# Cross-attention and expert FFN on one core: casts moved to GpSimd, attention's steps reordered, stack copies in 2 KB runs

## The chip, the core and the metric

The kernel runs on one core of a Trainium2 chip. Its engines are TensorE (PE, matrix multiply into PSUM), VectorE (DVE), ScalarE (ACT), GpSimd (POOL) and SyncE (SP, which here issues nearly all plain transfers). Each engine runs its own list of instructions in order and waits on semaphores. The metric is device time in microseconds for one launch, as the median of several runs.

## The reference

`x` and the context are (8, 512, 256), 16 heads of 16, hidden size 682, 8 experts of which each token takes 2.

```python
def xattn(x, k, v, w, b):            # k = v = context
    q = split(x) / 16 ** 0.25; k = split(k) / 16 ** 0.25
    p = softmax(einsum('bthd,bshd->bhts', q, k))
    return merge(einsum('bhts,bshd->bthd', p, v)) @ w.T + b
def ffn(x, Wg, W1, W2, W3):
    logits = x @ Wg.T
    gate = softmax(where(in_top_2(logits), logits, -inf))
    h = silu(einsum('bsd,ehd->bseh', x, W1)) * einsum('bsd,ehd->bseh', x, W2)
    return einsum('bsed,bse->bsd', einsum('bseh,edh->bsed', h, W3), gate)
x = x + xattn(layernorm(x), ctx, ctx, w_proj, b_proj)
x = x + ffn(layernorm(x), Wg, W1, W2, W3)
```

## The kernel before

**Numbers.** Many operands stand as two f16 parts: a high part (the value rounded to f16) and a low part (value minus high part, again f16). The normalised queries, the keys, the normalised rows `z` for the FFN and the expert weights are all split so. For each the high part is a copy with a cast, and the low part a subtraction behind it.

**Attention.** The eight batches go through a software pipeline of *slots*, 16 (`PER`) for a batch, each in two halves. Batch b's slot s stands at slot 16b + s; what is due for it at a constant `AT_...` (counted from its first slot, negative for what is prepared ahead) is issued when every engine's loop comes to that slot. So steps of three or four batches stand side by side in one stretch of 16 slots, which I call a frame. In a half slot PE makes the transposed scores of the batch eight slots behind (line 1284, for the exponential), the scores of the current batch (line 1271, for the row maximum), and, in the first half, four products of probabilities and values (line 1299); then at most one *misc* step: a transpose or small product whose half slot stands in `HALF_MISC`. ACT takes the exponential of 128x1024 (line 842); DVE takes the maximum of 128x1024 (line 973). Both read from three pairs of PSUM banks that the score products take in turn: a product waits for the reader of the product three before it. `max` is the misc step that transposes the maxima of a quarter of a batch (line 1313); ACT then copies them to `max_row` (line 859) and SP moves them into row 48 of each stack.

**Stacks.** The score products contract over `q_stack` and `k_stack`: three blocks of 16 rows (high, high and low part against high, low and high) in partitions 0 to 47 for the even heads and 64 to 111 for the odd ones, each row 8 pairs of heads x 512. Twelve transfers a batch (`k_part`, line 492, and `q_part`, line 497) copy them there from `k16` and `qt16` on SP's queue. Batch b's first score product waits for all twelve (line 1271's block).

**POOL's list.** In a frame POOL does, in this order of slots (mod 16): `pick_slots` (1), `inverse_root` for x (2), `scatter` with its 8 indirect transfers (2, line 474), `split_weights` 0 (3), `inverse_root` for z (4), low part of q (5), `split_weights` 1 (7), low part of z and its copy (8, lines 805 and 809), low part of the keys (12, line 694), `choose` (12, lines 700 to 718), `split_weights` 2 (14, lines 749 to 759). ACT makes the high part of the keys (line 914, slot 14), of q (line 927) and of z (line 931, slot 8). `choose` gives `sel16`, for which PE's misc step `prefix` waits (line 1352, slot 15).

**SP's list.** In the frame: weights out and the next weights in (slots 1, 9, 13), `x_in` and `v_ext` (5), `kt_in` and the keys' six stack transfers (10, both behind POOL's low keys), q's six (12), the maxima (2, 6, 10, 14), `x_res` and `x2` (0).

**FFN.** 36 tiles of 256 slots: gathered rows, three products for each pair of parts. The first six tiles (`EARLY`) are cut in 12 pieces each and stand in the half slots from 272 on, beside the last batch's attention; the others follow in plain loops. POOL adds each tile's two halves to the output with an indirect transfer (`add_rows`, line 769); for the early tiles those stand in its list at fixed half slots: tile 0's at 288 and 292 (slots 144 and 146).

Of the kernel before, what the change touches and what calls it, by code (L numbers as in the profile page):

```python
# [9 lines left out]
F16 = mybir.dt.float16  # L10
# [88 lines left out]
AT_CHOOSE = 44  # L99
# [4 lines left out]
AT_K_LO = -4  # L104
AT_K_PARTS = -6
AT_MAX_ROW = 2
AT_PICK = 49
AT_Q_HI = -13
AT_Q_LO = -11
AT_Q_PARTS = -4  # L110
AT_SCATTER = 50
AT_V_IN = 5
AT_WEIGH = 12
AT_W_LO = (3, 7, 14)
# [4 lines left out]
AT_X_RES = 16  # L119
AT_X_ROOT = -14  # L120
AT_Z_HI = 40
AT_Z_LO = 40
# [3 lines left out]
STEP_PREP = (-98, -96, -94, -92, -79)  # L126
# [3 lines left out]
HALF_MISC = sorted([(-23, 'turn_q', 0), (-20, 'turn_q', 1), (10, 'max', 0), (16, 'max', 1), (24, 'max', 2), (33, 'max', 3), (39, 'heads', 0), (43, 'heads', 1), (49, 'heads', 2), (55, 'turn', 0), (57, 'heads', 3), (59, 'turn', 1), (61, 'project', 0), (63, 'project', 1), (66, 'project', 2), (69, 'project', 3), (77, 'turn_z', 1), (79, 'turn_z', 0), (83, 'logits', 0), (85, 'turn_l', 0), (94, 'prefix', 0)])  # L130
# [140 lines left out]
def build(nc, xq_l, x_l, v_l, kT_l, wp_l, bias, wg_l, w12_l, w3_l, const, out):  # L271
    ctx = ExitStack()
    with ctx:
# [25 lines left out]
        run = sb("run", [P, E])  # L299

# [105 lines left out]
        s_small = sem("s_small")  # L406
        s_cst = sem("s_cst")
# [73 lines left out]
        def _(sp):  # L481
# [7 lines left out]
            def k_part(b, j, part):  # L489
                for par in range(2):  # L490
                    row = 64 * par + j * D
                    sp.dma_start(k_stack[b % 2][row:row + D, :, :], k16[part][:, par, :]).then_inc(s_kd, 16)

            def q_part(b, j, part):
                for par in range(2):
                    row = 64 * par + j * D
                    sp.dma_start(q_stack[b % 2][row:row + D, :, :], qt16[part][:, par, :]).then_inc(s_qd, 16)
# [174 lines left out]
        def _(pool):  # L672
# [112 lines left out]
            for slot in range(FIRST, LAST):  # L785
                for b in due(slot, AT_K_LO):
                    if b >= 1:
                        low_keys(b)
# [14 lines left out]
                for b in due(slot, AT_Z_LO):  # L803
                    pool.wait_ge(s_zh, b + 1)
# [26 lines left out]
        def _(act):  # L831
            act.wait_ge(s_con, 16)
# [64 lines left out]
            for slot in range(FIRST, LAST):  # L897
# [13 lines left out]
                for b in due(slot, AT_K_HI):  # L911
                    act.wait_ge(s_kin, (b + 1) * 16)
                    ge(act, s_kd, b * 96)
                    nc.scalar.copy(k16[0][:, :, :], kt_in[:, :, :]).then_inc(s_kh, 1)
# [13 lines left out]
                for b in due(slot, AT_Z_HI):  # L928
                    act.wait_ge(s_zn, (b + 1) * NT)
                    ge(act, s_sc, b * 128)  # L930
                    nc.scalar.copy(z_row[:, 0, :, 0:W // 2].bitcast(F16), z_n[:, :, :]).then_inc(s_zh, 1)
# [546 lines left out]
```

## Time and profile before

| | |
|---|---|
| median of 3 runs | 873.97 us (872.97 to 878.98) |
| the profiled execution | 874.99 us, span 873.1 us |
| PE busy | 784.8 us (90%) |
| DVE busy | 602.1 us (69%) |
| ACT busy | 557.6 us (64%) |
| POOL busy | 439.6 us (50%) |
| DMA queue of SP | 92448 packets, 148.76 MB, 60.0% of 16 engines |
| mean granted clock of PE | 0.992 |

Busy time is the time in which an engine ran an instruction; PE's matmuls overlap each other, and their ends are modelled. In the rows below, a time behind a group is the engine's idle time just before the instruction, with what ended it; "issue" is a wait that the profile puts down to nothing.

### The profile page before, as it was taken

What the parts mean: (1) busy time and instruction counts of PE and PEld (TensorE: products, weight loads), DVE (VectorE), ACT (ScalarE), POOL (GpSimd) and SP (SyncE); (2) the same over time, 40 slices, a digit from 0 to 9 for tenths busy, and PEclk for the clock granted to TensorE, in tenths of its full rate; (3) what the DMA queues carried; (4) which work ended last, traced back from release to release, by engine and by line L of the source; (5) the groups of instructions that cost most, each with busy time, mean ns of one, the idle gap of its engine ahead of it and who ended that gap; (6) DMA issues with size and microseconds to landing.
All of it is one profiled execution on the core that took longest, in us unless ns stands there. A gap on an engine that the chain in (4) does not pass through costs nothing.

```text
span 873.1 us, 20010 instructions
## 1 busy us (share of the span) xinstructions
PE 784.8 (90%) x6472; PEld 481.2 (55%) x6472; DVE 602.1 (69%) x1224; ACT 557.6 (64%) x970; POOL 439.6 (50%) x431
## 2 busy tenths in 40 slices
PE   0578898989989899897989899999999999999995
PEld 0112233333333333332326788888888888888884
DVE  4888888979888898899924557555555555555553
ACT  3369789888897988966884454444444444444442
POOL 4555435786777868675643665222224222222222
PEclk9999999999999999999999999999999999999998
DMA  8575756866659685674266699999997699383832
GB/s 184 179 191 167 202 124 225 188 217 157 189 209 188 215 170 190 182 161 169 106 195 225 190 252 299 293 308 271 267 261 160 161 250 255 57 251 49 250 41 25
DMA packets 105959, 167.57 MB, mean 192 GB/s; under 512 B 54688, under 2 KB 83232, under 8 KB 101280
## 3 DMA queue, kind: packets, MB, share of 16 engines
q1 hardware_dynamic: 92448, 148.76, 60.0%
q0 software_dynamic: 13440, 17.90, 10.6%
q8 instruction: 39, 0.64, 0.3%
q14 instruction: 32, 0.26, 0.1%
HBM read 119.75 MB, written 42.55 MB: 186 GB/s over the span
## 4 chain that ended last, share of the span: by engine, by line
PE 48%; ACT 2%; issue 1%; POOL 1%; DMA 0%; DVE 0%; POOLq 0%; ACTq 0%; DVEq 0%
PE ps L1376 10%; PE ps L1378 10%; PE ps L1380 10%; PE ps L1394 4%; PE ps L1396 4%; PE ps L1398 4%; PE ps L1299 2%; ACT probs L842 1%; PE ps L1403 1%; PE ps L1284 1%; POOL slots L474 1%; ACT z_n L847 1%; PE ps L1327 0%; PE ps L1338 0%; PE ps L1271 0%
## 5 line engine op out<-in xcount | busy, mean ns | idle before, releaser
L973 DVE TENSOR_REDUCE neg_max<-ps 128x2 f16<-128x1024 f32 x256 | 309.1, 1221 | 37.6 <-PE ps L1271 32.9
L842 ACT ACTIVATE probs<-ps 128x1024 f32<-128x1024 f32 x256 | 259.0, 1024 | 61.7 <-PE ps L1284 61.2
L769 POOL DMA_INDIRECT out<-y,aim x72 | 113.4, 1574 | 237.6 <-DVE y L1202 160.0
L1376 PE MATMUL ps<-zt,w 128*128 128x256 f16 x792 | 216.0, 273 | 1.4 <-issue 1.3
L1378 PE MATMUL ps<-zt,w 128*128 128x256 f16 x792 | 215.9, 273 | 0.0
L1380 PE MATMUL ps<-zt,w 128*128 128x256 f16 x792 | 215.9, 273 | 0.0
L876 ACT ACTIVATE silu<-ps 128x256 f32<-128x256 f32 x216 | 82.7, 383 | 183.4 <-PE ps L1380 173.8
L1183 DVE SCALAR_TENSOR_TENSOR hid<-ps,silu 128x256 f32<-128x256 f32 x216 | 91.7, 425 | 136.0 <-ACT silu L876 128.3
L1299 PE MATMUL ps<-probs,v_ext 128*32 128x512 f32 x1024 | 138.7, 613 | 5.3 <-ACT heads L910 4.4
L1271 PE MATMUL ps<-k_stack,q_stack 48*128 48x512 f16 x512 | 104.3, 406 | 35.4 <-ACT probs L842 17.8
L1284 PE MATMUL ps<-q_stack,k_stack 49*128 49x512 f16 x512 | 101.9, 396 | 7.3 <-DVE neg_max L973 7.1
L1394 PE MATMUL ps<-w,hid 128*128 128x256 f16 x360 | 98.1, 273 | 0.0
L1396 PE MATMUL ps<-w,hid 128*128 128x256 f16 x360 | 98.1, 273 | 0.0
L1398 PE MATMUL ps<-w,hid 128*128 128x256 f16 x360 | 98.1, 273 | 0.0
L1284 PEld LDWEIGHTS ps<-q_stack,k_stack 49*128 49x128 f16 x512 | 24.7, 93 | 113.0 <-issue 79.9
L1376 PEld LDWEIGHTS ps<-zt,w 128*128 128x128 f16 x792 | 77.5, 98 | 15.0 <-issue 5.3
L1378 PEld LDWEIGHTS ps<-zt,w 128*128 128x128 f16 x792 | 77.5, 98 | 9.0
L1380 PEld LDWEIGHTS ps<-zt,w 128*128 128x128 f16 x792 | 77.5, 98 | 9.0
L1190 DVE TENSOR_TENSOR hid<-hid 128x256 f16<-128x256 f32 x180 | 76.3, 424 | 1.3
L884 ACT CAST hid<-hid 128x256 f16<-128x256 f32 x180 | 72.0, 400 | 6.0 <-DVE hid L1183 2.4
L474 POOL DMA_INDIRECT slots<-z_row,slot_u x64 | 63.2, 987 | 24.4 <-issue 20.2
L759 POOL TENSOR_TENSOR w_lo<-w_in,w_hi 128x1408 f16<-128x1408 f32 (+1 forms) x24 | 70.7, 2946 | 2.0
(126 smaller groups left out, 908.0 us busy)
## 6 DMA issues: line engine op xcount, KB each, us to landing
w<-w_parts SPq DMA_DIRECT2D x36, 1408.0 KB
w<-w_parts SPq DMA_DIRECT2D x36, 768.0 KB
w_in<-in_w SPq DMA_DIRECT2D x16, 704.0 KB, 6.0
v_ext<-in_v SPq DMA_DIRECT2D x8, 1024.0 KB, 5.6
k_stack<-k SPq DMA_DIRECT2D x48, 128.0 KB, 5.3
q_stack<-qt SPq DMA_DIRECT2D x48, 128.0 KB, 5.0
w_in<-in_w SPq DMA_DIRECT2D x8, 768.0 KB, 5.0
w_parts<-w_hi SPq DMA_DIRECT2D x16, 352.0 KB, 2.3
```

The costliest lines, as they stand in the source:

```text
L769: nc.gpsimd.indirect_dma_start(out=out, out_offset=bass.IndirectOffsetOnAxis(ap=aim[frm][:, t, 0:1].bitcast(U32), axis=0), in_=y[frm][:, t ...
L842: nc.scalar.activation(probs[g % 2][:, j:j + 2, k, :], pair_banks[PLACE["exp", u] % 3], ACT.Exp, scale=0.25).then_inc(s_exp, 1)
L973: nc.vector.tensor_reduce(neg_max[b % 2][:, i, c:c + 3:2], pair_banks[PLACE["max", u] % 3], AX.X, ALU.max, negate=True).then_inc(s_red, 1)
L1271: mm = nc.tensor.matmul(to[:, par, :], q_stack[r][rows, a, i * P:(i + 1) * P], k_stack[r][rows, a, :], start=True, stop=True)
L1284: mm = nc.tensor.matmul(to[:, par, :], k_stack[r][rows, a, k * P:(k + 1) * P], q_stack[r][rows, a, :], start=True, stop=True)
L1299: mm = nc.tensor.matmul(pv_bank[32 * n:32 * n + 32, :], v_ext[b % 2][:, j, 4 * g + n, :], probs[g % 2][:, n, j, :], start=(j == 0), stop=( ...
L1376: nc.tensor.matmul(dst, w[:, kk, 1, cols], z16[:, kk, :], start=(kk == 0), stop=False)
L1378: nc.tensor.matmul(dst, w[:, kk, 0, cols], z16[:, 2 + kk, :], start=False, stop=False)
L1380: mm = nc.tensor.matmul(dst, w[:, kk, 0, cols], z16[:, kk, :], start=False, stop=(kk == 1))
L1394: nc.tensor.matmul(y_bank[t], h[1], w3[par][:, 0, m, :], start=first, stop=False, skip_group_check=True)
L1396: nc.tensor.matmul(y_bank[t], h[0], w3[par][:, 1, m, :], start=False, stop=False, skip_group_check=True)
L1398: nc.tensor.matmul(y_bank[t], h[0], w3[par][:, 0, m, :], start=False, stop=False, skip_group_check=True)
```

## The change

- The high part of the keys (batches 1 to 7) and of z (all batches) is made by POOL, just ahead of the low part, and no longer by ACT.
- POOL's order in a frame: `inverse_root` for x at slot 13 (was 2, in the frame after), low q 6 (was 5), high and low keys 9 (was 12, low alone), high and low z 10 (was 8, low alone), `split_weights` 2 at 12 (was 14), `choose` and `pick_slots` 15 (were 12 and 1 of the next frame).
- The misc step `max` 3 stands at half slot 32 (was 33).
- Two statistics of x on DVE move by one or more quarter slots, and the aggregate by one.
- `v_ext` and `x_res` are due a slot later and a slot earlier on SP; no other transfer of SP stands between the old place and the new.
- The host lays the keys and queries out so that two pairs of heads lie side by side in a partition: each stack transfer reads 64 partitions in runs of 2 KB (was 128 in runs of 1 KB).
- ACT runs one exponential of 128x1 before anything else.

```diff
-AT_CHOOSE = 44
+AT_CHOOSE = 47
-AT_K_LO = -4
+AT_K_LO = -7
-AT_PICK = 49
+AT_PICK = 47
-AT_Q_LO = -11
+AT_Q_LO = -10
-AT_V_IN = 5
+AT_V_IN = 6
-AT_W_LO = (3, 7, 14)
+AT_W_LO = (3, 7, 12)
-AT_X_RES = 16
-AT_X_ROOT = -14
-AT_Z_HI = 40
-AT_Z_LO = 40
+AT_X_RES = 15
+AT_X_ROOT = -19
+AT_Z_LO = 42
-STEP_PREP = (-98, -96, -94, -92, -79)
+STEP_PREP = (-98, -97, -93, -91, -78)
-HALF_MISC = sorted([... (33, 'max', 3), ...])
+HALF_MISC = sorted([... (32, 'max', 3), ...])
...
-                    sp.dma_start(k_stack[b % 2][row:row + D, :, :], k16[part][:, par, :]).then_inc(s_kd, 16)
+                    sp.dma_start(k_stack[b % 2][row:row + D, :, :], k16[part][64 * par:64 * par + 64, :, :]).then_inc(s_kd, 16)
...
                 for b in due(slot, AT_K_LO):
                     if b >= 1:
+                        pool.wait_ge(s_kin, (b + 1) * 16)
+                        ge(pool, s_kd, b * 96)
+                        nc.gpsimd.tensor_copy(k16[0][:, :, :], kt_in[:, :, :]).then_inc(s_kh, 1)
                         low_keys(b)
...
                 for b in due(slot, AT_Z_LO):
+                    pool.wait_ge(s_zn, (b + 1) * NT)
+                    ge(pool, s_sc, b * 128)
+                    nc.gpsimd.tensor_copy(z_row[:, 0, :, 0:W // 2].bitcast(F16), z_n[:, :, :]).then_inc(s_zh, 1)
                     pool.wait_ge(s_zh, b + 1)
...
         def _(act):
+            act.wait_ge(s_zero, 1)
+            nc.scalar.activation(warm_up[:, :], ones16[:, 0:1], ACT.Exp).then_inc(s_warm, 1)
+            act.wait_ge(s_warm, 1)
...
-                for b in due(slot, AT_Z_HI):
-                    act.wait_ge(s_zn, (b + 1) * NT)
-                    ge(act, s_sc, b * 128)
-                    nc.scalar.copy(z_row[:, 0, :, 0:W // 2].bitcast(F16), z_n[:, :, :]).then_inc(s_zh, 1)
...
-    x_q = np.asarray(x).reshape(B, T, PAIRS, 2, D).transpose(0, 1, 3, 4, 2)
+    x_q = np.asarray(x).reshape(B, T, PAIRS // 2, 2, 2, D).transpose(0, 1, 3, 4, 5, 2)
```

## Rows read from the trace of the kernel before

**Rows 1.** Busy time by stretch; columns: stretch, length, PE, PEld, DVE, ACT, POOL, PEclk, DMA.

```profile
257.50:310.57 53.07, 48.28 (x370) 16.98 (x370) 46.80 (x80) 45.70 (x59) 40.19 (x45) 1.00 0.71 195
...
528.00:858.00 330.00, 328.61 (x3002) 292.80 (x3001) 178.93 (x472) 158.41 (x427) 103.39 (x67) 1.00 0.81 207
```

**Rows 2.** What PE waited for, 26.7 to 460 us: total, times, longest.

```profile
PE ps L1271 <- ACT probs L842: 17.8, 38, 1.5
...
PE ps L1271 <- DMA q_stack<-qt: 1.0, 1, 1.0
PE ps L1271 <- issue: 0.9, 2, 0.7
```

**Rows 3.** Timeline of PE over a frame's end and the next one's start: start, length.

```profile
273.89 0.19 PE L1352 MATMUL ps<-sel,upper 128*128 128x32 f16 x1
...
277.04 0.39 PE L1271 MATMUL ps<-k_stack,q_stack 48*128 48x512 f16 x2 [0.66 <-issue]
...
278.90 0.39 PE L1313 MATMUL ps<-ident,neg_max 128*4 128x128 f16 x4
...
279.87 0.39 PE L1271 MATMUL ps<-k_stack,q_stack 48*128 48x512 f16 x2 [0.27 <-ACT probs L842]
...
283.78 0.39 PE L1271 MATMUL ps<-k_stack,q_stack 48*128 48x512 f16 x2 [0.69 <-ACT probs L842]
```

**Rows 4.** Timeline of ACT in the same frame.

```profile
254.47 1.03 ACT L931 CAST z_row<-z_n 128x1024 f16<-128x1024 f32 x1
...
280.20 0.56 ACT L859 COPY max_row<-ps 4x512 f16<-4x512 f16 x1
```

**Rows 5.** Timeline of POOL in the same frame.

```profile
250.12 2.87 POOL L759 TENSOR_TENSOR w_lo<-w_in,w_hi 128x1408 f16<-128x1408 f32 x1
255.58 2.14 POOL L805 TENSOR_TENSOR z_row<-z_n,z_row 128x1024 f16<-128x1024 f32 x1 [2.59 <-ACT z_row L931]
...
258.90 2.12 POOL L694 TENSOR_TENSOR k<-kt_in,k 128x1024 f16<-128x1024 f32 x1
263.10 0.19 POOL L700 CAST top_f<-top_e 128x8 f32<-128x8 uint32 x1 [2.08 <-DVE top_e L1018]
...
265.44 1.48 POOL L749 TENSOR_SCALAR w_in<-w_in 128x1536 f32<-128x1536 f32 x1
...
272.30 1.04 POOL L723 TENSOR_TENSOR ediff<-con,diff 128x4 f32<-128x4 f32 x1
...
275.16 0.20 POOL L681 TENSOR_TENSOR rstd<-mv,con 128x4 f32<-128x4 f32 x1
...
276.95 0.20 POOL L736 CAST z_row<-con 128x8 uint32<-128x8 f32 x1
```

**Rows 6.** Groups by line and shape: a cast on POOL; busy, mean ns, idle before.

```profile
L752 POOL CAST w_hi<-w_in 128x1408 f16<-128x1408 f32 x16 | 21.7, 1357 | 1.1
```

**Rows 7.** Timeline of SP and of POOL: loads of the third weights, and one's arrival.

```profile
97.85 0.47 SPq L502 DMA_DIRECT2D w_in<-in_w  x1
...
103.36 1.47 POOL L749 TENSOR_SCALAR w_in<-w_in 128x1536 f32<-128x1536 f32 x1 [12.21 <-DMA w_in<-in_w]
...
255.81 0.46 SPq L502 DMA_DIRECT2D w_in<-in_w  x1
```

**Rows 8.** Start of the program: timelines of ACT and DVE.

```profile
6.92 1.28 ACT L914 ACT_TABLE_LOAD   x1 [6.92 <-DMA kt_in<-in_k_t]
...
24.82 1.41 DVE L980 BATCH_NORM_STATS2 stats<-x_in 128x6 f32<-128x256 f32 x4 [9.06 <-DMA x_in<-in_x_q]
```

**Rows 9.** DMA view of 8 to 27 us: GB/s in 40 slices of 0.475 us.

```profile
GB/s 398 393 323 261 59 57 224 203 168 155 147 110 145 127 136 123 125 136 127 144 106 149 114 151 106 160 112 140 136 188 103 164 371 414 423 440 347 382 380 128
```

**Rows 10.** Last batch beside the early FFN tiles: timelines of POOL and of PE.

```profile
494.91 1.63 POOL L769 DMA_INDIRECT out<-y,aim  x1 [0.30 <-issue]
495.94 0.85 POOL L681 TENSOR_TENSOR rstd<-mv,con 128x4 f32<-128x4 f32 x1
...
500.72 0.52 PE L1338 MATMUL ps<-con,z_n 128*128 128x128 f32 x3 [1.86 <-ACT z_n L847]
```

More of the change, by code:

```diff
@@ L129 @@
 STEP_TOP_INDEX = 173
-HALF_MISC = sorted([(-23, 'turn_q', 0), (-20, 'turn_q', 1), (10, 'max', 0), (16, 'max', 1), (24, 'max', 2), (33, 'max', 3), (39, 'heads', 0), (43, 'heads', 1), (49, 'heads', 2), (55, 'turn', 0), (57, 'heads', 3), (59, 'turn', 1), (61, 'project', 0), (63, 'project', 1), (66, 'project', 2), (69, 'project', 3), (77, 'turn_z', 1), (79, 'turn_z', 0), (83, 'logits', 0), (85, 'turn_l', 0), (94, 'prefix', 0)])
+HALF_MISC = sorted([(-23, 'turn_q', 0), (-20, 'turn_q', 1), (10, 'max', 0), (16, 'max', 1), (24, 'max', 2), (32, 'max', 3), (39, 'heads', 0), (43, 'heads', 1), (49, 'heads', 2), (55, 'turn', 0), (57, 'heads', 3), (59, 'turn', 1), (61, 'project', 0), (63, 'project', 1), (66, 'project', 2), (69, 'project', 3), (77, 'turn_z', 1), (79, 'turn_z', 0), (83, 'logits', 0), (85, 'turn_l', 0), (94, 'prefix', 0)])
 FIRST, LAST = -27, PER * (B - 1) + 51
@@ L299, in build @@
         run = sb("run", [P, E])
+        warm_up = sb("warm_up", [P, 1])
         att = ctx
@@ L406, in build @@
         s_small = sem("s_small")
+        s_warm = sem("s_warm")
         s_cst = sem("s_cst")
@@ L496, in q_part @@
                     row = 64 * par + j * D
-                    sp.dma_start(q_stack[b % 2][row:row + D, :, :], qt16[part][:, par, :]).then_inc(s_qd, 16)
+                    sp.dma_start(q_stack[b % 2][row:row + D, :, :], qt16[part][64 * par:64 * par + 64, :, :]).then_inc(s_qd, 16)
             def load_weights(e, c):
@@ L911, in _ @@
                 for b in due(slot, AT_K_HI):
-                    act.wait_ge(s_kin, (b + 1) * 16)
-                    ge(act, s_kd, b * 96)
-                    nc.scalar.copy(k16[0][:, :, :], kt_in[:, :, :]).then_inc(s_kh, 1)
+                    if b == 0:
+                        act.wait_ge(s_kin, 16)
+                        nc.scalar.copy(k16[0][:, :, :], kt_in[:, :, :]).then_inc(s_kh, 1)
                 for i in range(NT):
@@ L1437 @@
     c = np.asarray(ctx_1024)
-    x_q = np.asarray(x).reshape(B, T, PAIRS, 2, D).transpose(0, 1, 3, 4, 2)
-    k_t = c.reshape(B, T, PAIRS, 2, D).transpose(0, 4, 2, 3, 1).reshape(B, P, 2, T)
+    x_q = np.asarray(x).reshape(B, T, PAIRS // 2, 2, 2, D).transpose(0, 1, 3, 4, 5, 2)
+    k_t = c.reshape(B, T, PAIRS // 2, 2, 2, D).transpose(0, 4, 5, 2, 3, 1).reshape(B, P, 2, T)
     v = np.zeros((B, P, NT, H, 32), np.float32)
```

## The prediction

> **What bounds the kernel now.** I read the stretches first. From 528 us to the end PE is busy 328.61 of 330 us: the FFN tiles run at PE's pace, and nothing in this change touches them [rows 1]. All that can move lies before. A steady attention frame, 257.5 to 310.57 us, has PE busy 48.28 of 53.07 us, DVE 46.80, ACT 45.70 and POOL 40.19 [rows 1]. So PE is the bound there as well, with 4.8 us of idle time in a frame; a faster ACT or a busier POOL matters only where PE waits for it. Then I read what PE waited for: 17.8 us for exponentials in 38 waits, 1.0 us for `q_stack`, 0.9 us in two waits that the profile calls issue [rows 2]. Last I read the frame's timelines, for the place of each wait and the slack of each engine's list [rows 3 to 5].
>
> **The change, part by part.** The sum is made against the profiled execution (874.99 us), which lies 1.0 us above the median of the three runs (873.97 us); the forecast is given against the median.
>
> *Casts off ACT.* ACT loses two casts of about 1.03 us in a frame [rows 4]. They pay only where an exponential is late for PE. The cast of z stands at 254.47 us and the keys' one 17 us behind it; PE's waits for exponentials in this frame stand at 279.87 us (0.27 us) and 283.78 us (0.69 us), in half slots where no misc step separates two score products, and there ACT itself had been waiting for PE [rows 3, 4]. What hides the casts is ACT's own slack, 7.4 us of 53.07 [rows 1]. I take 0. Other frames could hold some of it: the far end is all of the 17.8 us [rows 2], the near end is 0.
>
> *Casts onto POOL.* Two casts of 1024 at 1357 ns for 1408 [rows 6] are 0.99 us each, 2 us in a frame of which POOL idles 12.9 [rows 1]. The question is what is queued behind. PE's `prefix` at 273.89 us [rows 3] waits for `choose`, which now stands behind `split_weights` 2 and `inverse_root`. Worked from POOL's times [rows 5]: `split_weights` 1 ends at 250.12 + 2.87 = 252.99. High and low keys, 0.99 + 2.12, end at 256.1; high z, 0.99, and low z with its copy, 258.90 - 255.58 = 3.32, end at 260.4. The third weights are asked for at 255.81; the same load asked for at 97.85 had POOL working at 103.36, 5.5 us later [rows 7], so they are here at 261.3. The split takes 272.30 - 265.44 = 6.9, to 268.2; `inverse_root` 276.95 - 275.16 = 1.8, to 270.0; `choose` 265.44 - 263.10 = 2.3, to 272.3. That is 1.6 us ahead of `prefix`: cost 0. If the cover is gone, each us of lateness is one us of PE in each of six frames. `pick_slots` waits for DVE behind `prefix` in both orders, so `scatter` gains at most `inverse_root`'s 1.8 us, and the z root behind it waits for DVE's statistics: worth 0.
>
> *`max` 3 from half slot 33 to 32.* The second half slot of slot 0 is now empty. A score product of the following half must wait for the exponential begun in this one. With the transposes between (278.90 us) the wait at 279.87 was 0.27 us; with nothing between, as in the next slot, it is 0.69 us at 283.78 [rows 3]. PE's work is the same, so the step costs 0.42 us. The copy of the maxima (0.56 us, at 280.20 [rows 4]) also moves from behind that exponential to ahead of it; the transposes end shortly before the product, so I add 0.1 of it. That is 0.5 us in a frame. It happens for batches 0 to 6; batch 7's has no score product beside it, and batch 6's falls where DVE builds the tile table and is late anyway, so I count six: +3.0 us. Ends: 0, if later waits absorb it, and 7 x (0.42 + 0.56) = 6.9.
>
> *Statistics of x, `v_ext`, `x_res`.* DVE's pieces move by a quarter slot or two past one maximum, whose result PE needs two half slots later; the transfers pass no other. 0.
>
> *Keys' transfers earlier.* POOL finishes the low keys at 256.1 instead of 258.90 + 2.12 = 261.0 [rows 5]; SP has just asked for the third weights (255.81 [rows 7]), so the keys' six leave some 4.7 us earlier and are through before q's six, which stay where they are behind the second maxima. The wait at 277.04 (0.66 us, called issue [rows 3]) is that of a batch's first score product, like the 1.0 us for `q_stack` [rows 2]. Both issue waits go: -0.9 us. The 1.0 us is batch 1's, whose keys were not late: it stays. Ends: 0 and -1.9.
>
> *2 KB runs.* At the start the queue carries stack packets alone from its seventh to its thirty-second slice. The first two slices reach 224 and 203 GB/s, then the rate falls to between 103 and 188, about 130, though the packets are the same size; `x_in` behind them runs at 371 to 440 [rows 9]. A cost for each packet would hold from the first slice on, so I read a limit on bytes at the rows that are written, and take 0. The other end is a doubled rate: q's six transfers (786 KB at 130 GB/s, 6.0 us) in 3.0 us, with batch 1's `x_in`, for which DVE waits until 24.82 us [rows 8], 2.6 us earlier beyond the next term, and the 1.0 us of batch 1 gone: -3.6 us together.
> By the Trainium skill, page "SBUF — State Buffer", section "Door 1: The DMA port swizzle", sixteen neighbouring partitions reach only 4 of the 16 ports of 27.2 GB/s, 109 GB/s for one transfer whatever its runs; that page speaks against this edit, its sum is +3.2 us where a price for each packet would give -0.4, and the slices near 130 GB/s, with two transfers overlapping, agree with it.
>
> *Early exponential.* The table load (1.28 us at 6.92 us [rows 8]) moves ahead of the keys' arrival, so the high keys are ready 1.28 us earlier. The normalised q is not, as it waits for POOL. The queue is at 59 and 57 GB/s in slices five and six [rows 9], nearly 1 us that the keys can fill; q's transfers then meet less backlog. -0.3 us, ends 0 and -0.8.
>
> *The adds of the first FFN tile.* `pick_slots` of batch 6 moves from slot 145 to 143, past the add at slot 144, and holds it until PE's `prefix` is done. The add then stands between the pick and `scatter`. One add takes 495.94 - 494.91 = 1.03 us up to the next operation, which takes 0.85 instead of 0.20 us [rows 5, 10]: 1.0 to 2.0 us, and I take 1.4. Behind `scatter` come tile 0's second add and batch 7's root, for which ACT's z and PE wait, at 500.72 already for 1.86 us [rows 10]: +1.4 us.
>
> Sum: 0 + 0 + 3.0 + 0 - 0.9 + 0 - 0.3 + 1.4 = +3.2 us: 878.2 us against the profiled execution, 877.2 us as a median.
>
> **The rivals.**
> *ACT was the hidden bound.* Then the waits for exponentials (17.8 us [rows 2]) shrink with its load. For it: 38 waits are on ACT. Against: those shown stand where ACT had idled. If 8 to 18 us go and the rest of the sum holds, 869 to 859 us. Chance 0.12, of which 0.08 below 865.2.
> *The stack copies double their rate.* -3.6 on the sum: 873.6 us. For it: packets were at the highest rate when few were in flight. Against: the fall within a microsecond [rows 9]. Chance 0.18.
> *The moved `max` 3 is absorbed* by the frame's other waits: +0.2, 874.2 us. Chance 0.10.
> *`choose` comes too late (slower).* Its place is `prefix`. It decides once `split_weights` 2 starts later than 261.3 + 1.6 = 262.9 us: a load of 7.1 us instead of 5.5, now that the keys' transfers leave right behind it. A cast at the subtraction's price (2.1 us) would bring POOL itself only to 262.7. Two us over are 6 x 2 = 12 us: 889 us; one is 883. Chance 0.10.
> *Main case*, 873 to 881 us. Chance 0.50.
>
> **How the numbers follow.** The likeliest case gives 877.2 us. About 1% (8.7 us) is what a measurement of this kernel can tell from no change. Faster than 865.2 takes the larger part of the first rival and a little for what I don't see: 0.10. Slower than 882.7 takes nearly all of the late `choose` and a little of the main case's upper bounds (6.9 + 2.0): 0.11. Within 1%: 0.79. The range 868 to 883 us holds the main case, the doubled copies, the absorbed step and the edge of the other two.
>
> **What would show it.** In the changed kernel: the score product of half slot 2 waits about 0.7 to 0.8 us for an exponential in every frame; no issue wait at a batch's first score product from batch 2 on; stack packets of 2 KB take about twice as long and the DMA rate in 12 to 20 us stays near 130 GB/s; DVE starts on batch 1's statistics at about 24.5 us; `prefix` never waits for POOL; PE's wait for batch 7's z is near 3.3 us. I am wrong if PE's waits for exponentials fall by several us, if the early stack copies end 2 us sooner, or if `prefix` waits.

## The result, and the profile after

| | before | after |
|---|---|---|
| median (4 runs each, same chip) | 874.42 us (872.97 to 878.98) | 885.65 us (883.39 to 887.93) |
| ratio, 95% interval | | 1.0105 [1.0081, 1.0130] |
| the profiled execution, its span | 874.99 us, 873.1 us | 886.15 us, 884.3 us |
| PE busy | 784.8 us | 787.2 us |
| ACT / POOL busy | 557.6 / 439.6 us | 543.9 / 453.5 us |

The change costs 11.2 us, where 3.2 were forecast. The span (first to last instruction of the profiled execution) grew by 11.2 us too, so the two traces hold the whole loss.

**Where it is.** I looked first for the place. The last group of products of probabilities and values stands at the same point of the work in both kernels, at the end of the steady attention. Timelines of PE, of the kernel before and then of the changed one (start, length):

```profile
470.72 1.06 PE L1299 MATMUL ps<-probs,v_ext 128*32 128x512 f32 x8
```

```profile
471.27 1.07 PE L1305 MATMUL ps<-probs,v_ext 128*32 128x512 f32 x8
```

So at the start of that group the changed kernel is 0.55 us behind, and 10.7 us are lost after it. I call what follows this group the *tail*: 402.4 us of the span before, 413.0 after. Busy time by stretch there (columns as in [rows 1]), before and after:

```profile
500.00:520.00 20.00, 19.28 (x195) 17.11 (x196) 10.68 (x38) 11.57 (x30) 13.35 (x18) 1.00 0.99 247
520.00:540.00 20.00, 20.00 (x185) 17.93 (x184) 16.77 (x56) 10.01 (x27) 11.88 (x13) 1.00 1.04 308
```

```profile
499.00:502.50 3.50, 0.41 (x4) 0.12 (x2) 0.00 (x0) 2.04 (x5) 1.27 (x3) 1.00 0.96 287
502.50:505.90 3.40, 3.22 (x15) 2.52 (x16) 1.92 (x5) 2.57 (x8) 0.00 (x0) 0.50 0.87 297
505.90:523.00 17.10, 14.19 (x140) 12.20 (x137) 8.46 (x31) 7.24 (x19) 10.06 (x8) 1.00 0.77 185
523.00:529.80 6.80, 3.96 (x29) 2.93 (x30) 1.85 (x9) 0.00 (x0) 5.12 (x16) 0.50 0.78 253
540.00:858.00 318.00, 316.51 (x2892) 282.13 (x2891) 172.29 (x453) 152.45 (x412) 96.03 (x62) 1.00 0.83 211
```

PE idles in two places and then runs at a granted clock of 0.50 (1.2 GHz instead of 2.4) for 3.4 and 6.8 us. From 540 us on the tiles run as before. What PE waited for from 460 us on (total, times, longest), the two longest of after; the longest of before was the 1.86 us for `z_n` of [rows 10]:

```profile
PE ps L1358 <- POOL sel L717: 5.7, 1, 5.7
PE ps L1344 <- ACT z_n L857: 3.3, 1, 3.3
```

**The bill.** `prefix` of batch 7 waits 5.75 us for the `sel16` of `choose`. The wait for `z_n` is 3.27 us instead of 1.86 [rows 10]: +1.4. In a half-clock stretch the work takes twice its time, so half the busy time is lost: 3.22 / 2 = 1.6 and 3.96 / 2 = 2.0, an estimate. Together 10.8 us, of 10.7.

**How it comes about.** Timeline of POOL in the changed kernel; the adds are those of tile 0 (483.61 and 496.89), tile 1 (507.29 and 509.22) and tile 2 (520.03 and 521.92). In [rows 10] tile 0's second add starts at 494.91 us.

```profile
482.83 0.46 POOL L732 TENSOR_TENSOR pick<-hot,pos 128x32 f32<-128x32 f32 x2 [5.15 <-DVE pos L1048]
483.61 1.81 POOL L770 DMA_INDIRECT out<-y,aim  x1 [0.32 <-issue]
...
496.89 1.61 POOL L770 DMA_INDIRECT out<-y,aim  x1 [0.30 <-issue]
...
507.29 1.63 POOL L770 DMA_INDIRECT out<-y,aim  x1 [6.86 <-issue]
509.22 1.56 POOL L770 DMA_INDIRECT out<-y,aim  x1 [0.30 <-issue]
...
520.03 1.58 POOL L770 DMA_INDIRECT out<-y,aim  x1 [4.79 <-DMA out<-y,aim]
521.92 1.53 POOL L770 DMA_INDIRECT out<-y,aim  x1 [0.30 <-issue]
522.89 0.76 POOL L701 CAST top_f<-top_e 128x8 f32<-128x8 uint32 x1
...
525.45 0.25 POOL L717 TENSOR_TENSOR sel<-hot 128x32 f16<-128x32 f32 x1
```

The first lines are the foreseen step: the pick waits 5.15 us with tile 0's first add behind it, and the scatter and the second add follow 2.0 us later than before (1.4 us, if the 0.55 us by which all of it is behind is taken off). The rest was not foreseen. Timeline of SP, before and then after: the loads of w1 and w2 (1.4 MB each) and, at 498.71 us, one of w3 (768 KB):

```profile
496.46 0.36 SPq L546 DMA_DIRECT2D w<-w_parts  x1
```

```profile
496.64 0.36 SPq L547 DMA_DIRECT2D w<-w_parts  x1
498.71 0.34 SPq L557 DMA_DIRECT2D w<-w_parts  x1
...
509.62 0.34 SPq L547 DMA_DIRECT2D w<-w_parts  x1
```

The second add starts at 496.89 us, 0.25 us *behind* the load; in the kernel before it started 1.55 us ahead of it (494.91 against 496.46). I call this distance the add's *lead*. The DMA view of the changed kernel, of 498 to 502 us and then of 502 to 506 us, splits the packets by queue (hardware_dynamic is SP's, software_dynamic is GpSimd's). The last two fences give the add's time from issue to landing, after and then before:

```profile
q1 hardware_dynamic: 92, 1.04, 93.8%
```

```profile
q1 hardware_dynamic: 182, 1.08, 66.5%
q0 software_dynamic: 143, 0.13, 20.6%
```

```profile
out<-y,aim POOLq DMA_INDIRECT x1, 9.6
```

```profile
out<-y,aim POOLq DMA_INDIRECT x1, 4.2
```

From 498 to 502 us not one packet of the add moves. From 502 to 506 us its packets (143 of 1 KB or less) share the time with the last 27 of the 1.4 MB load, of 11 KB each, and with 126 of the w3 load, of 6 KB. It lands 9.6 us after its start, against 4.2 us in the kernel before. Tile 1's adds wait for it (`add_rows` waits for all adds of the tile before) and start at 507.29 us. The second of them, at 509.22 us, is 0.4 us *ahead* of the next load, and that is not enough: the view of 511 to 514 us has no packet of GpSimd's queue, and 520.03 us is when POOL goes on, with the add landed. `choose` of batch 7 stands behind tile 2's adds, because the change moved it from slot 156 to 159. Its input, the indices that DVE finds, was complete at 515.3 us, 4.8 us before PE went idle for it:

```profile
515.12 0.16 DVE L1024 FIND_INDEX8 top_e<-top,logit 128x8 uint32<-128x8 f32 x1
```

In the kernel before, `choose` stood ahead of tile 2's adds; its `sel16` was ready at 514.1 us, 2.3 us before `prefix`.

**The other steps.** PE's waits over the attention, 26 to 460 us, after (compare [rows 2]): exponentials take 2.9 us more, and no issue wait at a batch's first score product is left.

```profile
PE ps L1277 <- ACT probs L852: 20.7, 35, 1.5
```

PE in the half slots of `max` 3 and of the next slot (compare 279.87 and 283.78 in [rows 3]), and the start of the program on ACT and DVE (compare [rows 8]):

```profile
277.37 0.39 PE L1277 MATMUL ps<-k_stack,q_stack 48*128 48x512 f16 x2 [0.81 <-ACT probs L852]
...
281.28 0.39 PE L1277 MATMUL ps<-k_stack,q_stack 48*128 48x512 f16 x2 [0.69 <-ACT probs L852]
```

```profile
0.71 1.28 ACT L840 ACT_TABLE_LOAD   x1 [0.71 <-PEq L1476]
...
6.97 1.04 ACT L924 CAST k<-kt_in 128x1024 f16<-128x1024 f32 x1 [4.77 <-DMA kt_in<-in_k_t]
```

```profile
24.11 1.41 DVE L986 BATCH_NORM_STATS2 stats<-x_in 128x6 f32<-128x256 f32 x4 [8.12 <-DMA x_in<-in_x_q]
```

### The profile page after: what moved, and what is told of

The parts are those of the page before. It is cut to its first block and busy times, and to the rows that moved or that the text cites. A ratio compares the mean times of both kernels' runs of the same rounds, so it can differ in the third digit from the quotient of the medians.

```text
span 884.3 us, 20011 instructions
## 1 busy us (share of the span) xinstructions
PE 787.2 (89%) x6472; PEld 483.5 (55%) x6472; DVE 602.1 (68%) x1224; ACT 543.9 (62%) x956; POOL 453.5 (51%) x446
## 5 line engine op out<-in xcount | busy, mean ns | idle before, releaser
L1277 PE MATMUL ps<-k_stack,q_stack 48*128 48x512 f16 x512 | 104.2, 406 | 35.4 <-ACT probs L852 20.7
L1290 PEld LDWEIGHTS ps<-q_stack,k_stack 49*128 49x128 f16 x512 | 24.7, 93 | 109.0 <-issue 69.1
```

The costliest lines, as they stand in the source:

```text
L1277: mm = nc.tensor.matmul(to[:, par, :], q_stack[r][rows, a, i * P:(i + 1) * P], k_stack[r][rows, a, :], start=True, stop=True)
L1290: mm = nc.tensor.matmul(to[:, par, :], k_stack[r][rows, a, k * P:(k + 1) * P], q_stack[r][rows, a, :], start=True, stop=True)
```

## The experiments

The theory: the two moved steps `pick_slots` (batch 6) and `choose` (batch 7), among the adds of the first tiles, are the loss; casts, stack runs and `max` 3 play no part in it. Ratios are to the kernel before on the same chip, with 95% intervals. The kernel before itself ran between 872.5 and 882.3 us in these comparisons, so differences of 2 us between versions are at the edge of what they can tell. In the diffs `B - 1` is batch 7 and `B - 2` batch 6; the other batches stay where the changed kernel has them.

**1. `choose` of batch 7 alone at its old slot**

```diff
                 for b in due(slot, AT_CHOOSE):
-                    choose(b)
+                    if b < B - 1:
+                        choose(b)
+                for b in due(slot, 44):
+                    if b == B - 1:
+                        choose(b)
```

> The changed kernel with one thing put back: batch 7's choose stands at its old slot (156), ahead of the two adds of FFN tile 2, which wait for earlier adds to land. Theory (choose of batch 7 is caught behind adds whose landing is 8 to 10 us late): PE's wait of 5.75 us at prefix goes, and with it the 6.8 us at half clock right behind it, worth 3.4 us; PE's wait for batch 7's z (3.3 us) stays. Time 875 to 879 us against 885.7 for the changed kernel. Rival 1 (POOL is overloaded by the casts, so it would be late with choose wherever it stands): prefix still waits 2 to 5 us, 881 to 885 us. Rival 2 (the loss is spread over attention's frames): no change, 885 us.

Measured 879.91 us, ratio 1.0041 [1.0014, 1.0069]. Batch 7's `prefix` no longer waits for POOL, and the wait for `z_n` stays at 3.3 us. PE waits 1.8 us for heads behind it, and 6.8 us at half clock follow with PE busy for 6.1 of them, where 3.4 us had followed in the changed kernel; the forecast had no such stretch left, and its 879 us were just missed. With `pick_slots` late, `choose`'s place is worth some 0.6% of the 1.05. Neither of the expected rivals' times came (881 to 885, 885 us).

**2. `pick_slots` of batch 6 alone at its old slot**

```diff
                 for b in due(slot, AT_PICK):
-                    pick_slots(b)
+                    if b != B - 2:
+                        pick_slots(b)
+                for b in due(slot, 49):
+                    if b == B - 2:
+                        pick_slots(b)
```

> The changed kernel with another thing put back: batch 6's pick_slots stands at slot 145 again, behind tile 0's first add. Theory: the scatter and tile 0's second add start about 2 us earlier, the add gets ahead of the 1.4 MB weight load of an FFN tile instead of behind it and lands in about 5 us instead of 10; PE's wait for z falls from 3.3 to about 1.9 us; tile 1's and 2's adds are earlier, so batch 7's choose, though still behind tile 2's adds, is late by 1 to 4 us instead of 5.75. Time 876 to 882 us. Rival 1 (POOL's casts): the wait for z stays near 3.3 us and the time near 885. Rival 2 (spread over the frames): 885 us.

Measured 876.95 us, ratio 1.0009 [0.9983, 1.0034]: the loss is gone with this step alone, though `choose` still stands late. So the two steps don't add up: `choose` is late only when the adds are. Timeline of POOL and SP: the second add starts 1.5 us ahead of the load and lands after 4.5 us, tile 2's adds follow each other, and `choose` is in time (1 to 4 us of lateness had been expected):

```profile
494.77 1.62 POOL L770 DMA_INDIRECT out<-y,aim  x1 [0.30 <-issue]
500.06 1.62 POOL L770 DMA_INDIRECT out<-y,aim  x1 [1.75 <-issue]
...
511.25 1.55 POOL L770 DMA_INDIRECT out<-y,aim  x1 [0.31 <-issue]
512.73 0.27 POOL L701 CAST top_f<-top_e 128x8 f32<-128x8 uint32 x1
```

```profile
496.24 0.36 SPq L547 DMA_DIRECT2D w<-w_parts  x1
```

**3. Both at their old slots**

The two edits above together.

> The changed kernel with both put back: batch 7's choose at slot 156 and batch 6's pick_slots at 145. Theory: prefix does not wait, z waits about 1.9 us, no stretch of half clock behind them; time 872 to 875 us, level with the kernel before, as what is left of the change gains 0.8 us up to 425 us. Rival 1 (POOL's casts): 879 us or more. Rival 2 (spread over the frames): 885 us.

Measured 879.14 us, ratio 1.0024 [1.0000, 1.0048]; the profiled execution took 875.95 us, with a `z_n` wait of 1.8 us and no wait for `sel16` in the tail. It cannot be told from experiment 2. The median is at the edge of the first rival (879 us or more), not in the expected 872 to 875 us; the traces, and experiments 4 and 7 to 9, speak against that rival.

**4. The kernel before with these two constants alone**

```diff
-AT_CHOOSE = 44
+AT_CHOOSE = 47
-AT_PICK = 49
+AT_PICK = 47
```

> The kernel before with only choose and pick_slots at slot 47 of their batch, as in the changed kernel; casts on ACT, 1 KB runs, max 3 at 33, split_weights and inverse_root where they were. Theory: this alone makes the loss, since the place of pick_slots and choose among the adds is all that matters: z waits 3.3 us, prefix of batch 7 waits 4 to 6 us, half clock behind them; 883 to 887 us. Rival 1 (POOL's casts): 874 to 876 us. Rival 2 (spread over the frames by max 3 and the rest): 874 us.

Measured 888.30 us, ratio 1.0134 [1.0086, 1.0182]. No cast moved to GpSimd, no 2 KB run, no moved `max`, and the whole loss is there: the tail of the profiled execution is 10.2 us longer than before (10.7 in the changed kernel). The other 2.9 us of that execution were lost before 473.6 us; it started later and had three stretches at half clock there instead of two. Tile 0's second add started 0.04 us ahead of the load and landed after 9.1 us. What PE waited for from 460 us on:

```profile
PE ps L1352 <- POOL sel L716: 5.8, 1, 5.8
PE ps L1338 <- ACT z_n L847: 3.2, 1, 3.2
```

**5. Experiment 3 with `max` 3 at half slot 33**

```diff
-HALF_MISC = sorted([... (32, 'max', 3), ...])
+HALF_MISC = sorted([... (33, 'max', 3), ...])
```

> The changed kernel with choose (batch 7) at slot 156 and pick_slots (batch 6) at slot 145 again, as in the last-but-one experiment, and also max 3 back at half slot 33. The prediction charged max 3 at half slot 32 with 0.5 us in each of six frames (3.0 us). The two traces gave 0.34 us more for the half-slot pair (2.83 us before, 3.17 us after). Theory (max 3 costs 0.34 x 7 = 2.4 us and later waits give nothing back): ratio to the kernel before 0.997 to 1.000, that is 2.4 us below the version with max 3 at 32 (1.0024 of the kernel before), and the pair of half slots 2.8 us again. Rival (the step is absorbed by the frame's other waits): no difference to the version with max 3 at 32, ratio 1.001 to 1.003, frame period 52.4 us as before.

Measured 875.71 us, ratio 0.9999 [0.9976, 1.0023]. That is 2.2 us below experiment 3 (1.0024), as 7 x 0.34 = 2.4 us has it, but the intervals overlap: not settled by the times. Nor by where the attention ends in the two traces (469.45 against 470.73 us), since experiment 3 had 10.2 us at half clock before that point and this one 3.4. The trace shows the pair back at the old wait, and the total of the waits for exponentials at 17.1 us (20.7 in the changed kernel):

```profile
279.74 0.39 PE L1285 MATMUL ps<-k_stack,q_stack 48*128 48x512 f16 x2 [0.27 <-ACT probs L860]
```

**6. Experiment 3 with the old 1 KB runs and host layout**

```diff
-                    sp.dma_start(k_stack[b % 2][row:row + D, :, :], k16[part][64 * par:64 * par + 64, :, :]).then_inc(s_kd, 16)
+                    sp.dma_start(k_stack[b % 2][row:row + D, :, :], k16[part][:, par, :]).then_inc(s_kd, 16)
...
-    x_q = np.asarray(x).reshape(B, T, PAIRS // 2, 2, 2, D).transpose(0, 1, 3, 4, 5, 2)
...
+    x_q = np.asarray(x).reshape(B, T, PAIRS, 2, D).transpose(0, 1, 3, 4, 2)
```

> The changed kernel with choose (batch 7) and pick_slots (batch 6) at their old slots, and the stack copies in runs of 1 KB from 128 partitions with the host layout of before. Theory (the copies are limited by bytes, so the runs are worth nothing): packets of 1 KB take 100 to 150 ns again, half of the 2 KB ones, DVE starts on batch 1's statistics at 24.1 us (within 0.3 us), and the time is within 1 us of the version with 2 KB runs (ratio to the kernel before 1.001 to 1.003). Rival (a price for each packet): DVE starts at 26 us or later, the time is 2 to 3.6 us above it (ratio 1.005 to 1.007).

Measured 877.59 us, ratio 1.0021 [0.9997, 1.0044], against 1.0024 with 2 KB runs: no difference, and the rival's 1.005 lies outside the interval. DVE starts on batch 1's statistics at 24.99 us; in the ten traces with 2 KB runs it starts between 24.11 and 25.55 us. The time expected (24.1 us) was too narrow, the rival's 26 us is not there. The profiled execution waited 2.5 us for batch 1's `q_stack` and ran 17.1 us at half clock from 69.5 us on, which accounts for most of its 882.99 us. The other three traces with 1 KB runs waited 1.0 us or less there, so the runs alone don't bring that wait.

```profile
24.99 1.41 DVE L994 BATCH_NORM_STATS2 stats<-x_in 128x6 f32<-128x256 f32 x4 [9.27 <-DMA x_in<-in_x_q]
```

**7. The changed kernel with both casts on ScalarE again**

```diff
-                        nc.gpsimd.tensor_copy(k16[0][:, :, :], kt_in[:, :, :]).then_inc(s_kh, 1)
...
-                    nc.gpsimd.tensor_copy(z_row[:, 0, :, 0:W // 2].bitcast(F16), z_n[:, :, :]).then_inc(s_zh, 1)
...
+                    nc.scalar.copy(k16[0][:, :, :], kt_in[:, :, :]).then_inc(s_kh, 1)
+                for b in due(slot, 40):
...
+                    nc.scalar.copy(z_row[:, 0, :, 0:W // 2].bitcast(F16), z_n[:, :, :]).then_inc(s_zh, 1)
```

> The changed kernel with both casts (keys, z) on ScalarE again at their old slots; everything else as changed. Theory (the loss is the order of pick_slots and choose among the adds of the first FFN tiles): GpSimd has 2 us less to do in a frame and it changes nothing: 884 to 887 us, ratio 1.009 to 1.013, PE's wait for sel16 at batch 7's prefix stays at 5 to 6 us, the wait for z_n at 3.3 us. Rival (the casts on GpSimd make choose late): the wait at prefix shrinks by 2 us or more, ratio 1.007 or less. A second rival (ACT's casts made exponentials late, and moving them off was a hidden gain): the waits for exponentials between 30 and 425 us grow by several us and the time is above 888 us.

Measured 885.35 us, ratio 1.0097 [1.0068, 1.0127]: the loss stays without any cast on GpSimd. But the profiled execution, at 879.12 us, was one of the two short ones of eight and had no wait at `prefix`. Tile 0's second add was held here too (0.3 us behind its load, landed after 9.0 us), but tile 1's second add got 1.5 us ahead of the next load and landed after 4.3 us:

```profile
509.43 1.56 POOL L770 DMA_INDIRECT out<-y,aim  x1 [0.32 <-issue]
...
514.52 1.58 POOL L770 DMA_INDIRECT out<-y,aim  x1 [0.16 <-issue]
```

```profile
510.90 0.34 SPq L547 DMA_DIRECT2D w<-w_parts  x1
```

**8. The same kernel once more, to see the other group**

> The same kernel as the one with both casts on ScalarE again, once more. Its eight runs fell in two groups: 877.9 and 879.1 us, and six of 884.6 to 890.1 us, and the profiled one was of the lower group: there tile 1's second add started at 509.43 us, 1.5 us ahead of the next 1.4 MB load (asked for at 510.90), and landed at 513.7; PE did not wait at batch 7's prefix. In the changed kernel it started at 509.22 us, 0.4 us ahead of the load (509.62), and landed at 519.3. Theory (which of the two groups a run falls in is decided by whether this add gets ahead of the load): if the profiled run is of the upper group (884 us or more), the add's start is less than 1 us ahead of the load, it lands at 518 us or later and PE waits 5 to 6 us at prefix; if it is of the lower group (below 880.5), it is 1.4 us or more ahead, lands by 515 and PE doesn't wait there. Rival (the groups differ by the granted clock or the start of the program alone): the two numbers don't go with the time of the profiled run.

Measured 884.54 us (883.61 to 888.89), the profiled execution 884.88 us. The load went out 0.2 us ahead of the add, and POOL went on, with the add landed, only at 519.23 us. `prefix` waited 3.7 us, less than the 5 to 6 expected. That is 2 us less than in the changed kernel, as a cost of the casts would have it; but experiment 4, which has its casts on ScalarE too, waited 5.8 us, and what differs is that this add landed after 8.1 us and that of the changed kernel after 10.0:

```profile
510.36 1.56 POOL L770 DMA_INDIRECT out<-y,aim  x1 [0.30 <-issue]
519.23 1.57 POOL L770 DMA_INDIRECT out<-y,aim  x1 [3.94 <-DMA out<-y,aim]
```

```profile
510.16 0.34 SPq L547 DMA_DIRECT2D w<-w_parts  x1
```

```profile
PE ps L1356 <- POOL sel L717: 3.7, 1, 3.7
```

One kernel, two times 5.8 us apart, and the lead of an add over a load goes with them. With two traces that is a match, not a proof; the next experiment tries the cause itself.

**9. The load held until the adds have landed**

```diff
                     load_rows(k + 2, half + 1, par, least + 2)
+                    if least == 0:
+                        sp.wait_ge(f_add, 32)
                     load_up(k + 2, half + 1, par, least + 2)
```

> The changed kernel, with one wait more on SyncE alone: the load of the first and second weights for tile 2 (1.4 MB, asked for at 496.6 us in the changed kernel) is asked for only when both adds of tile 0 have landed. GpSimd's list is that of the changed kernel. In the trace of the changed kernel tile 0's second add starts at 496.89 us and its packets of 1 KB move only at 502 to 505 us, when the load's packets of 11 KB are through; it lands at 506.5 us. Theory (the add is held by the load in front of it): it lands about 5 us after its start, at 502 us, the next pair of adds starts at 502 to 504 us instead of 507.3 and lands by 509, so add (2, first) no longer holds choose, and PE's wait for sel16 at batch 7's prefix falls from 5.8 us to at most 1.5 us; the late load may cost PE up to 5 us at tile 2's first products, so the whole may be anywhere from 878 to 886 us. Rival (the add is slow of itself or through the scatter in front of it): it still lands at 506 us or later and the wait at prefix stays at 5 to 6 us; the time rises above 886 us.

Measured 895.67 us, ratio 1.0210 [1.0166, 1.0253]. The disputed point came out: issued at 498.25 us behind the same scatter, the add took 3.9 us to land instead of 9.6 (DMA view, 498.2 to 502.2 us, no other queue has a packet there):

```profile
q0 software_dynamic: 192, 0.26, 39.8%
out<-y,aim POOLq DMA_INDIRECT x1, 3.9
```

So neither the add nor the scatter is slow; the loads hold it. The edit moves both loads back, the 1.4 MB one to 503.61 us and the one of w3 behind it to 505.44 us, so it doesn't tell their shares apart; by the packets above, the first kept the add from starting and the second shared its last 4 us. The price was misjudged: PE waited 15.4 us, which I put down to the late weights, not up to 5, and the time lies where the rival had it (above 886 us). `prefix` of batch 7 had no wait for `sel16`, but everything behind the load had shifted, so that says nothing.

```profile
509.62 0.37 PE L1384 MATMUL ps<-zt,w 128*128 128x256 f16 x1 [15.41 <-issue]
```

Read across all traces, the second adds of tiles 0 and 1 that start within 1.6 us of a 1.4 MB load fall in groups by their lead over it:

| lead of the add | adds | landed after |
|---|---|---|
| 1.47 to 1.58 us | six: before, experiments 2, 3, 5 (tile 0), 1, 7 (tile 1) | 3.8 to 4.9 us |
| 1.44 us | experiment 6 (tile 0) | 6.2 us |
| 0.40 us ahead to 0.30 us behind | seven: changed kernel (both), 1, 4, 7 (tile 0), 8 (both) | 8.1 to 10.0 us |

Why being 0.4 us ahead doesn't help can be read from the packets. With nothing in their way the first packets of an add move 2.2 us after its start (at 497.1 us in the kernel before, at 500.4 us in this experiment), and the first of a load 1.0 us after it is asked for (at 497.6 and 510.6 us in the changed kernel). So an add needs a lead of about 1.2 us to move its first packet first; that is an estimate from these four times.

**10. Experiment 5 with batch 6's scatter at slot 149, behind batch 7's z root**

```diff
                 for b in due(slot, AT_SCATTER):
-                    finish_rows(b)
-                    scatter(pool, b)
+                    if b != B - 2:
+                        finish_rows(b)
+                        scatter(pool, b)
+                for b in due(slot, 53):
+                    if b == B - 2:
+                        finish_rows(b)
+                        scatter(pool, b)
```

> As the version with both steps at their old slots and max 3 at half slot 33, and also batch 6's finish_rows and scatter moved from slot 146 to slot 149, behind batch 7's z root. In the kernel before, PE waits 1.9 us for batch 7's normalised z, because the root stands behind the pick, an add and the scatter on GpSimd. Theory (the z wait is a GpSimd order cost): the wait for z_n falls below 1 us and the time is 1 to 2 us below the version without this move. Rival (the early FFN work takes the freed time up, since the scattered rows or the tile table come later, or other waits follow): same time within 1 us, or slower if tile rows of batch 6 are needed earlier than they land.

Measured 882.09 us, ratio 1.0066 [1.0042, 1.0091]. The wait for `z_n` fell to 0.9 us as expected, but the time rose by 0.7%, as the rival had it: 6.1 us at `prefix` came in its place, since tile 1's adds now stand behind the scatter, start at 505.26 us, and low z and `choose` slip with them.

```profile
PE ps L1371 <- POOL sel L717: 6.1, 1, 6.1
PE ps L1357 <- ACT z_n L870: 0.9, 1, 0.9
```

**11. Experiment 5 with the z root between the sixth and seventh scatter transfer, and tile 0's second add ahead of the scatter**

```diff
             for c in range(2):
                 for i in range(NT):
+                    if between and (c, i) == (1, 2):
+                        between()
...
+                    if b == B - 2:
+                        add_rows(0, 0, 1, 0)
                     finish_rows(b)
-                    scatter(pool, b)
+                    scatter(pool, b, z_root if b == B - 2 else None)
```

> The version with both steps at their old slots and max 3 at half slot 33, and in GpSimd's list tile 0's second add ahead of batch 6's scatter, and batch 7's z root between the sixth and the seventh of the scatter's eight transfers. The root's input was there at 491.65 us where GpSimd stood idle before it, and the root started at 494.65 us behind the scatter and the add; PE waited 1.8 us for z_n. Theory: the root starts within 0.6 us of its input, the wait for z_n falls from 1.8 us to at most 0.5 us, the adds of tile 1 still start at 499 to 500 us and no wait at prefix comes back: 1.3 to 1.8 us below the version without it, ratio to the kernel before 0.996 to 1.000. Rival (a chain of adds and loads next to it decides): prefix or the heads product waits again, ratio 1.003 or more.

Measured 876.69 us, ratio 0.9990 [0.9965, 1.0015]: no gain that can be told. The profiled execution (881.53 us) waited 4.5 us at two `prefix` steps of the attention.

**12. The kernel before with that edit alone**

The edit of experiment 11 to GpSimd's list, made to the kernel before.

> The kernel before with only the GpSimd edit of the last experiment: tile 0's second add ahead of batch 6's scatter, batch 7's z root between its sixth and seventh transfer. Theory: the wait for z_n (1.9 us before) goes to at most 0.5 us, nothing else moves: ratio 0.998 (1.4 to 1.9 us less). If this comes out as low as the version above, the rest of the change (casts on GpSimd, keys' transfers earlier, early exponential) is worth nothing; by the prediction's terms it would be worth -1.2 us. Rival: the freed time is lost at a later wait, ratio 1.000 or more.

Measured 877.87 us, ratio 1.0009 [0.9986, 1.0031]. The wait for `z_n` went from 1.9 to 0.9 us, and 1.8 us for heads came up behind it. My estimate was at fault: I had set two absolute times of different executions against each other. Counted from the last group of products of probabilities and values, the root's input comes at +24.6 us and the root starts at +24.7 in experiments 10 to 12 alike, and the root of experiment 5 started at +25.2: there was 0.5 us to gain, and 0.6 us more in the root's first operation, which takes 0.84 us behind an add and 0.20 us here. The idle time before the root shows that it now waits for its input:

```profile
500.00 0.20 POOL L683 TENSOR_TENSOR rstd<-mv,con 128x4 f32<-128x4 f32 x1 [1.94 <-DVE mv L993]
```

**The tails side by side.** Where the attention ends in a trace varies by 12 us, from start to start of nearly the same code, so I take the rest of each span by itself (time of the last group of products of probabilities and values, rest of the span, and the rest against the kernel before):

| trace | group at | tail | against before |
|---|---|---|---|
| before | 470.72 | 402.4 | |
| changed kernel | 471.27 | 413.0 | +10.7 |
| 1, `choose` back | 471.40 | 406.7 | +4.3 |
| 2, `pick_slots` back | 470.59 | 403.5 | +1.1 |
| 3, both back | 470.73 | 403.4 | +1.0 |
| 4, before with both moved | 473.62 | 412.6 | +10.2 |
| 5, as 3, `max` 3 back | 469.45 | 403.7 | +1.3 |
| 6, as 3, 1 KB runs | 478.75 | 402.4 | 0 |
| 7 and 8, casts back (short, long group) | 471.97, 472.38 | 405.3, 410.6 | +2.9, +8.2 |
| 9, loads held | 472.62 | 421.5 | +19.1 |
| 10, scatter late | 466.95 | 409.4 | +7.0 |
| 11, 12, root in the scatter | 478.12, 475.30 | 401.5, 402.4 | -0.9, 0 |

One trace each is little, but the loss is in the tail wherever `pick_slots` stands at its new slot, and nearly gone wherever it does not, except where another edit makes tile 1's adds late (10).

No version beats the kernel before by more than can be told. The best of those that keep the change is experiment 5, equal to it; by the two ratios (0.9999 and 1.0105) it is some 1% faster than the change as it stands.

## Why the prediction was wrong

The sign was right, the size and most of the place were not: +11.2 us for +3.2, outside the range. Of the +3.2 us, the sum had put +1.8 in the start and the attention (where the traces show 0.55) and +1.4 in the tail (where they show 10.7). So the sign is partly luck: the sum's largest term, `max` 3, is not what made the kernel slower.

*The failed step is "The adds of the first FFN tile".* It gave +1.4 us for the pick holding the add, through the scatter and the root to PE's wait for `z_n` "near 3.3 us". That came out to the tenth: 3.27. The 1.4 had been picked between 1.0 and 2.0 us, so the tenth is luck, the mechanism is not. The step ended there: what waits for the landing of the adds, and what stands behind the root in POOL's list, was in the sum at nothing, without a reason. It left out three things. The second add, now 2.0 us later, starts behind a 1.4 MB load and lands 9.6 us after its start, not 4.2 (experiment 9 shows the loads to be the cause). Each tile's adds wait for the last tile's, so POOL is held. And `choose` of batch 7 had itself been moved behind tile 2's adds: the prediction checked it against `split_weights` and the root in a steady frame, and not against the adds of the last one. Together 5.75 us at `prefix` and, with the longer `z_n` wait, 3.6 us at half clock. The load that mattered had stood 1.55 us behind the second add in the kernel before, so a delay of 2.0 us was enough.

*The rival "`choose` comes too late"* named the right wait and side, with a chance of 0.10, but its place was six attention frames and its cause the third weights' load. In the first five frames of the changed kernel `sel16` is ready 0.7 to 1.0 us ahead of `prefix` (1.6 forecast) and PE does not wait. The cover is thin: the traces of the experiments that have the changed kernel's whole order there show none or up to two waits, of 0.4 to 1.5 us in total, and once 4.5 us (experiment 11). That is a part of the rival, worth 0.5% of the time at most where it showed, and no part of the loss between these two traces. Of the three signs of being wrong that the prediction named, this one showed: `prefix` waited, though in the last frame alone.

*The clock* was in no term. It costs 1.6 + 2.0 us in the tail; the first stretch begins 0.2 us and the second 2.8 us before the wait ends, and both outlast it.

*`max` 3:* +3.0 forecast as 0.5 in six frames. The trace gives 0.34 (the product's wait is 0.81 instead of 0.27, part of which later work takes back), and experiment 5 is 2.2 us faster, within its error. The wait is there as forecast, somewhat smaller; what it costs the whole kernel is not settled.

*Casts:* 0 for ACT holds: ACT lost 13.7 us of work and PE's waits for exponentials did not shrink (17.8 to 20.7 us; 17.1 in experiment 5, where `max` 3 is at its old place). The first rival is out. 0 for POOL holds as far as the times tell (experiments 5 and 7); the cast of 128x1024 takes 1.04 us there where 0.99 was forecast.

*Keys' transfers and early exponential:* the issue waits went, and at 471 us the kernel is 0.55 us behind where the terms for `max` 3 (+3.0), the keys (-0.9) and the exponential (-0.3) gave +1.8. Each trace has two stretches of 3.4 us at half clock before that point, so the clock is no part of the 0.55. Other starts of nearly the same code differ by more, so the two small terms are not told apart.

*2 KB runs:* 0 holds within the error of experiment 6, and the second rival is out. From 12 to 20 us the DMA engines moved 129 to 153 GB/s in the ten traces with 2 KB runs and 133 to 143 in the four with 1 KB; nowhere did the rate double.

## What to carry to other kernels

A step moved in a list issued in order has to be followed to the end of the program: the last round often has neighbours (here, the adds of the next stage) that the steady rounds have not, and a check in a steady round says nothing of it. Write down by how much each small transfer precedes the next large one. Here a lead of 1.5 us was enough and one of 0.4 us was not, and losing it doubled the landing time and fed a chain of waits. When comparing two executions, count times from a common point of the work, and look for stretches at half clock before it.

## What the runs showed of the hardware

- An indirect add of 128 rows of 1 KB through GpSimd's queue landed after 3.9 us with no other queue's packet beside it (experiment 9), after 3.8 to 4.9 us with a 1.4 MB load asked for 1.47 to 1.58 us later, and after 8.1 to 10.0 us with the load asked for between 0.30 us before its start and 0.40 us after it (table behind experiment 9). In the changed kernel no packet of it moved from 498 to 502 us, while 92 of the load's 11 KB packets did.
- The first packet of an add moved 2.2 us after its start, that of a load 1.0 us after it was asked for (497.1, 500.4, 497.6 and 510.6 us above).
- An idle PE was followed by a lower clock, not always for the same time. In the changed kernel waits of 3.27 and 5.75 us were followed by 3.4 and 6.8 us at a granted clock of 0.50; in experiment 1 the same wait of 3.3 us was followed by 6.8 us. In the kernel before, with 1.86 us at the same place, it stayed at 1.00. But shorter waits are no safety: a wait of 1.75 us for heads, at the end of the attention, was followed by 3.4 us at half clock in the changed kernel and by none in the kernel before. Stretch of the changed kernel:

```profile
458.20:461.60 3.40, 3.40 (x18) 1.45 (x11) 0.00 (x0) 1.33 (x2) 0.00 (x0) 0.51 1.00 360
```

- Copies from one part of the on-chip memory to another, into 16 partitions each, ran at 129 to 153 GB/s from 12 to 20 us whether their packets were of 2 KB or of 1 KB; the median packet took 181 to 253 ns at 2 KB and 119 to 141 ns at 1 KB.
